# A graph network on one core: GpSimd issues the second four gathers of a group only once the running step's spread scores are out

## The reference

```python
z = (x @ W).reshape(n, HEADS, ODIM)            # HEADS = 4, ODIM = 64
el = jnp.sum(z * al, axis=-1)
er = jnp.sum(z * ar, axis=-1)
e = leaky_relu(el[src] + er[dst], 0.2)
ex = jnp.exp(e - segment_max(e, dst)[dst])
alpha = ex / segment_sum(ex, dst)[dst]
out = elu(segment_sum(z[src] * alpha[:, :, None], dst) + x + b)
```

## Time and profile before

| | us |
|---|---|
| three runs | 5960.23, 5965.95, 5992.97 (median 5965.95) |
| the profiled execution's own time | 5953.5 |
| its span, first to last instruction | 5951.7 |
| mean granted TensorE clock | 0.726 of full speed |
| layer 5, from L1387 of group 3 to that of group 50 | 4181.6 to 4900.7 |
| layer 6, the same | 5083.5 to 5802.8 |

### The profile page before, as it was taken

One profiled execution on the slowest core, in us unless ns is written; L12 is line 12 of the kernel. 1 busy time (PEld: TensorE's weight loads), 2 busy tenths in 40 slices (PEclk: granted clock), 3 DMA queues, 4 the chain that ended last, 5 costly groups with the idle time before them and its releaser, 6 DMA issues.

```text
span 5951.7 us, 60656 instructions
## 1 busy us (share of the span) xinstructions
PE 3434.0 (58%) x14500; PEld 2353.8 (40%) x14501; DVE 2011.9 (34%) x4393; ACT 1158.3 (19%) x3026; POOL 2914.6 (49%) x3013
## 2 busy tenths in 40 slices
PE   4777777755556444454444744445656664665566
PEld 2554445434334333343333433333444443444343
DVE  3666666511111111111111411113444445444446
ACT  1333333210001000010000100004332333233233
POOL 2344444046664666646666266663544543454450
PEclk6887778777767777787667767777766666766766
DMA  5454545122222232222222122222333332333330
GB/s 170 141 145 139 143 137 145 35 75 87 81 84 71 87 90 85 85 82 87 86 81 82 55 87 84 86 83 64 94 90 92 92 87 66 89 91 91 91 93 24
DMA packets 280482, 546.80 MB, mean 92 GB/s; under 512 B 72515, under 2 KB 161655, under 8 KB 280223
## 3 DMA queue, kind: packets, MB, share of 16 engines
q0 software_dynamic: 140416, 391.24, 23.1%
q1 hardware_dynamic: 139807, 152.86, 8.5%
HBM read 512.47 MB, written 31.37 MB: 91 GB/s over the span
## 4 chain that ended last, share of the span: by engine, by line
another core or an unknown queue 39%; PE 32%; issue 11%; DVE 11%; ACT 3%; DVEq 2%; SPq 1%; DMA 1%; POOL 1%; ACTq 1%; POOLq 0%
PE ps L627 9%; PE ps L711 7%; PE ps L534 3%; PE ps L499 2%; PE ps L872 2%; DVE rows L1425 2%; PE ps L852 1%; PE ps L822 1%; PE ps L634 1%; PE ps L814 1%; DVE inv L1531 1%; ACT norm L1020 1%; ACT rows L1037 1%; PE ps L486 1%
## 5 line engine op out<-in xcount | busy, mean ns | idle before, releaser
L1819 POOL DMA_INDIRECT rows<-table,src_idx x2912 | 2875.5, 987 | 2709.0 <-issue 865.6
L627 PE MATMUL ps<-rows,attr 128*128 128x256 f32 x3328 | 1066.3, 490 | 188.6 <-issue 93.1
L627 PEld LDWEIGHTS ps<-rows,attr 128*128 128x128 f32 x3328 | 824.1, 254 | 394.7 <-issue 215.2
L1317 DVE TENSOR_TENSOR acc<-acc,ps 128x256 f32 x208 | 87.7, 422 | 2035.0 <-PE ps L634 1532.2
L634 PE MATMUL ps<-ident,rows 128*128 128x128 f32 x416 | 110.9, 356 | 1151.7 <-ACT rows L1037 931.6
L634 PEld LDWEIGHTS ps<-ident,rows 128*128 128x128 f32 x416 | 48.8, 165 | 1235.1 <-ACT rows L1037 984.5
L711 PE MATMUL ps<-rows,w_roots 128*128 128x260 f32 x832 | 329.5, 551 | 35.6 <-DVE rows L1425 35.3
L711 PE MATMUL ps<-rows,attr 128*128 128x260 f32 x832 | 325.0, 544 | 35.3 <-DVE rows L1425 35.3
L1353 DVE TENSOR_TENSOR attr<-iota,local 128x1024 f32<-128x1024 f32 x208 | 254.3, 1224 | 204.9 <-issue 136.2
L1037 ACT ACTIVATE rows<-ps,mean_of 128x256 f32<-128x256 f32 x156 | 73.8, 473 | 1240.2 <-remote 826.0
L499 PE MATMUL ps<-rT,attr 128*128 128x272 f32 x832 | 283.1, 470 | 52.3 <-DMA rT<-table 25.8
(11 more groups left out here) (226 smaller groups left out, 4310.8 us busy)
## 6 DMA issues: line engine op xcount, KB each, us to landing
rT<-table SPq DMA_DIRECT2D x416, 136.0 KB
rows<-table,src_idx POOLq DMA_INDIRECT x2912
high_rows<-in_tiles SPq DMA_DIRECT2D x156, 256.0 KB
table<-rows SPq DMA_DIRECT2D x24, 512.0 KB, 2.9
table<-rows SPq DMA_DIRECT2D x12, 528.0 KB, 3.0
pens<-pen_rows SPq DMA_DIRECT2D x52, 96.2 KB
pens<-pen_rows SPq DMA_DIRECT2D x104, 48.1 KB
attr_parts<-acc SPq DMA_DIRECT2D x9, 416.0 KB
```

Source lines behind the costliest of these rows:

```text
L627: ins = mm(node_ps[par % 2], sum_hot[:, par % 2, k, :], src_rows(l, par)[:, k, 0:D], start=k == 0, stop=k == T - 1)
L1819: pool.indirect_dma_start(src_rows(l, par)[:, k, :], None, tables[l][:, :], bass.IndirectOffsetOnAxis(ap=src_idx[:, g * T + k:g * T + k + ...
```

## The change

In the two 4-head layers GpSimd gets one more wait, in the middle of each group but the first: before the fifth of its eight gathers it waits until `er_ready` stands at g, that is, until PE has spread the scores of group g-1. The number of gathers, their sizes and every other engine's instructions stay the same.

```diff
                     for k in range(T):
+                        if kind == "gat" and g > 0 and k == T // 2:
+                            wait_alone(pool, er_ready, NG * (l - 5) + g)
                         pool.indirect_dma_start(
                             src_rows(l, par)[:, k, :], None, tables[l][:, :],
                             bass.IndirectOffsetOnAxis(ap=src_idx[:, g * T + k:g * T + k + 1], axis=0)
```

## The result

The changed kernel takes **5875.82 us** (median; 5864.48 to 5892.23), the kernel before 5964.59 us beside it: ratio **0.985**, 95% interval [0.982, 0.987]. It is 1.5% faster; 4.1% was forecast. The profiled execution took 5864.48 us against 5953.5, 89 us less.

A forecast was written before the change was run, and what follows sets the result against it. PE's late release at L1387, 5.27 us a step, was taken as the bound. Steps of 12.81 instead of 15.30 us save 117.0 and 117.2 us, starts 3.9 and 5.0: 243 off 5953.5, stated as 5715, range 5650 to 5810.

The forecast's parts named there:

- What bounds the kernel: At L1387 in the 4-head layers: PE's release comes late with the gathers, 5.27 us of a 15.30 us step.
- The release comes 2.15 us behind the last gather: At L1387: `er_ready` follows the end of the gather stream by a fixed 2.15 us, not the start of L675.
- GpSimd stops at 0.75 + 9.91 = 10.66 us, released by L675: GpSimd's step from L1387: restart 0.75 us after the release, then eight gathers in 9.91 us, until the next wait.
- With gathers running, PE's ends of the scans still reach DVE in 0.32 us, so I take nothing: At L681 and L1425: gathers now early in the step were costed at no delay to DVE or PE.
- The sum: 2 x 47 steps save 117.0 and 117.2 us, the layers' starts 3.9 and 5.0: together 243 us, 4.1%.
- the hold: At L1387: PE's release of the spread scores comes late while gathers run, 5.27 us a step.
- 10.66 + 2.15 = 12.81: New step in the 4-head layers: GpSimd's stream plus the release's distance behind it, 12.81 us against 15.30.
- the 243: Total forecast saving in us over both 4-head layers, steps and starts, 4.1%.
- (d): Costed at nothing: gathers in the first 5.7 us of a step, where GpSimd was silent before 3.05 us.
- Rival 2: At L1387: hold of its own length or another cause, step 14.6 to 15.3, 5880 to 5955 us; chances 0.11 and 0.10.
- Rival 3: At the step's head, L681's result held behind eight gathers: slower, step 20.5 us, 6442 us; chance 0.07.
- The rule on the port pair: GpSimd and VectorE lock each other, PE never waits; by it moving gathers gives back next to nothing.

The follow-up runs named there:

- p1: Kernel before, gathers of groups 4 to 51 left out in both 4-head layers, on an occasion with the hold: 5353.2 us against 5907.4.
- p2: Kernel before, last two of each group's eight gathers left out in groups 4 to 51, with the hold: 5618.88 us against 5907.4.
- p7: Changed kernel with a second wait, gathers in two streams, six behind the spread scores and two behind the carry: 5680.12 us against 5913.5.
- p4: Changed kernel with the two small products of L686 done six times over, with the hold: 6054.7 us against the kernel before's 5907.4.
- p3: Changed kernel with a second wait, so that the eight gathers fall into two streams of four: 5749.37 us, ratio 0.973 to the kernel before.
- p6: Kernel before with the scores spread in 8 products instead of 24, with the hold: 5878.23 us against 5913.53.
- e1: Kernel before, gathers of groups 4 to 51 left out in both 4-head layers, on an occasion without the hold: 4708.92 us against 4770.2.
- p5: Changed kernel with a second wait, gathers in two streams, five behind the spread scores and three behind the carry: 5721.54 us, ratio 0.967.

## Why the prediction was right or wrong, point by point

- **What bounds the kernel** (a release of PE that comes late with the gathers, 5.27 us a step): right, and by `p1` shown: without the gathers it is gone, on the very occasion that has it.
- **The release comes 2.15 us behind the last gather**: right in kind, with 1.85 us after the change, 1.8 us for a stream of six (`p2`; 1.4 in `p7`), 1.0 for four and 0.8 for two.
- **GpSimd stops at 0.75 + 9.91 = 10.66 us, released by L675**: right, 10.49 us in the timeline.
- **"With gathers running, PE's ends of the scans still reach DVE in 0.32 us, so I take nothing"**: this is the step that failed. It looked at one release, L686's, and was right on it (0.26 us after the change, too). The next two of PE, behind L693 and L711, fall due 1.3 and 2.4 us later in the same stream and were held, as `er_ready` had been. The sum took the hold to be a thing of `er_ready`, the last link of the circle, with nothing behind it. It can take other releases of PE that fall due as the stream goes on, and behind L1414 2.45 us of chain are still to come. With that term and the measured distance, 10.49 + 1.85 + 2.45 = 14.79 stands where 10.66 + 2.15 = 12.81 stood. The mean step was 14.57, and 94 steps of 1.76 us are 165 us lost of the 243.
- **The trace of the kernel before already showed a held L693.** This stands just ahead of the earlier trace rows, in the second step of layer 5:

```profile
4149.54 0.34 PE L693 MATMUL ps<-one,carry_th 1*32 1x1 f32 x4 [2.91 <-DVE carry_th L1406]
4150.73 0.95 POOL L1819 DMA_INDIRECT rows<-table,src_idx  x1 [0.30 <-issue]
4154.28 0.35 DVE L1414 SCALAR_TENSOR_TENSOR ps<-pens,ps 32x128 f32<-32x128 f32 x1 [4.70 <-remote]
```

  L693 had ended at 4149.88, and L1414 came 4.40 us later, 2.60 us behind the last gather. L686's release in the same step came 1.94 us late (products to 4146.62, L1400 at 4148.56). There the gathers run at the head of the step, which is where the change puts them in every step: the 0.32 us of (d) was read in a step with another order.
- **Rival 2** gave the right time (14.6 us, 5880) by luck, through the wrong mechanism: the hold at L1387 did not keep its length, it vanished. Its mark, L1387 5 us behind L675 with GpSimd silent, is in no row after the change.
- **Rival 3** had the right mechanism in the wrong place: it put the hold at L681, where 20.5 us would have followed. With the stream at the head of the step, a release caught earlier in the chain costs more: L693 14.6 us, L686 (`p4`) 16.4 us. `p4` is slower than the kernel before.
- **The rule on the port pair** of the Trainium skill ("SBUF — State Buffer", section "SBUF: two separate sides") says that PE never waits on anyone. PE's own products took no longer here (L675 0.76 us with gathers beside it and without), and so the trace doesn't contradict the rule, but it doesn't reach this case: what is late is other engines' sight of PE's work, and taking the gathers away gives back 5.8 us a step.
- **What could not be seen in the one profile**: that the hold depends on the occasion. All runs shown ahead of the prediction had it. Where it is missing, the change makes the kernel 0.3% slower.

**What stays open.** What makes an occasion one or the other: the kernel before took 4773 and, later, 5914 us on the same chip, so it isn't the chip alone. Nor is it known what starts the hold: not the stream's age (`p3`), not the burst of products (`p6`). `p1` takes away the gathers' issue, their transfers and their landings together, so it doesn't say which of these holds a release. That PE's update is late, rather than one engine slow to see it, is argued from DVE and ACT going on within 0.04 us of each other after two different releases; no run separates these.

## What to carry to other kernels

When a wait at the end of a circle vanishes by moving work, list every release that falls due while the moved work runs and give each the price of the old wait plus the chain behind it; here the hold went to another release, and the step gained only what was left. A single release that comes through unhindered says nothing on the one a microsecond later. And before building on a wait that no instruction explains, run the kernel before once more on another occasion: here its time moved by 20% and the change's sign with it.

## What the runs showed of the hardware

- The same program took 4770 to 4776 us on three occasions and 5907 to 5967 us on four, steps of 10.16 and 15.3 us in the two 4-head layers. Without gathers the step is 9.5 us on either kind (9.51 and 9.54), though the whole of `p1` is still 644 us longer than `e1`: the other layers lose time as well.
- On the occasions with the hold, releases of PE that fall due while GpSimd's indirect gathers stream can be seen late by DVE, ACT and GpSimd. Those that were held in the steps shown came 0.8 us (a stream of two gathers, `p7`), 1.0 us (three in `p5`, four in `p3`), 1.4 to 1.8 us (six, `p7` and `p2`) and 1.7 to 2.2 us (eight, from `p4` to the kernel before) behind the end of the last. Others in the same streams came at once (L686's in the change, L698's in `p3`), and at the starts of the layers two came late while gathers still ran (4144.39 and 5051.42).
- SyncE's pair of small loads of L1737 takes longer from the first's start to the second's end in such a hold. One row of the kernel before and one of the change, in which no gather runs at that point:

```profile
4406.62 3.79 SPq L1737 DMA_DIRECT2D gat_pen_row<-pen_ends  x2
```

```profile
4411.00 1.41 SPq L1737 DMA_DIRECT2D gat_pen_row<-pen_ends  x2
```

- The traces with the hold keep fewer records of semaphore updates, 28,490 and 28,892 for the two kernels against 70,521 and 70,648 without it. The missing ones go with the gathers, as the hold does: from group 3 to group 50 of layer 5 the kernel before kept 3,247 records with the hold and 8,793 without, and with no gathers `p1` and `e1` kept 3,337 each. Whether that is a cause or a companion is not shown. The Trainium skill, "NOTIFIC — the notification-queue block", section "7.1 Overflow: three behaviours, one of which stalls the engine", says that records can be dropped when a ring is full, and that inside the block a crowded record path holds its producers back rather than lose a record. A hold by the recording itself would fit both observations; no run here tests it, since every execution that was timed was also recorded.
